# Three routed MLPs of an audio tower: tiles in twos on TensorE, with products ordered by row height

## The reference, cut to what matters

```
l1f, l3f:  Y = (silu(X W_gate) * (X W_up)) W_down          192 -> 2 x 512 -> 192
l3a:       Y = gelu(X W1 + b1) W2 + b2                     192 -> 768 -> 192
```

## Time and profile before

| | |
|---|---|
| device time, median of 3 runs | 2312.69 us (2310.74 to 2312.94) |
| the profiled execution, first to last instruction | 2358.7 us |
| TensorE busy in it | 1698.8 us (72%) |
| VectorE, ScalarE, GpSimd busy | 1290.5 (55%), 1022.7 (43%), 343.4 (15%) |
| mean granted TensorE clock, share of full speed | 0.840 |

### The profile page before, as it was taken

The page is one execution under the profiler, slowest core; times in us unless marked ns, Lnnn a source line. Parts: engine busy times, 40 slices in busy tenths (PEclk is TensorE's granted clock), DMA queues, the critical chain, the costliest instruction groups (busy, mean ns, idle before and its releaser), DMA issues. The chain is left out here.

```text
span 2358.7 us, 35978 instructions
## 1 busy us (share of the span) xinstructions
PE 1698.8 (72%) x12150; PEld 1375.5 (58%) x12166; DVE 1290.5 (55%) x2688; ACT 1022.7 (43%) x2115; POOL 343.4 (15%) x415
## 2 busy tenths in 40 slices
PE   3588879856760489966499686664893698469995
PEld 2265657745650355545489563443683598369995
DVE  6588963361137879968622468997316211642223
ACT  4466753312234568865112147873322254312221
POOL 0000000006640000001143100000000342034431
PEclk9799979977885589986699797775996699689998
DMA  3200000214450000000466300000004453446775
GB/s 85 71 18 19 21 23 9 49 50 128 136 164 16 2 7 7 5 1 12 140 214 212 108 4 8 7 4 1 13 1 127 135 179 118 130 139 223 223 218 191
DMA packets 137245, 189.82 MB, mean 80 GB/s; under 512 B 51661, under 2 KB 111213, under 8 KB 137069
## 3 DMA queue, kind: packets, MB, share of 16 engines
q1 hardware_dynamic: 116289, 146.91, 20.3%
q0 software_dynamic: 15360, 36.72, 5.4%
q10 hardware_dynamic: 5420, 3.91, 0.6%
HBM read 150.21 MB, written 33.68 MB: 78 GB/s over the span
## 5 line engine op out<-in xcount | busy, mean ns | idle before, releaser
L989 DVE TENSOR_TENSOR 36_l3f_mlp_hidden<-36_l3f_mlp_gate,36_l3f_mlp_first 128x512 f32<-128x512 f32 x51 | 35.1, 688 | 185.0 <-ACT 36_l3f_mlp_gate L967 101.0
L882 PE MATMUL 36_l3f_mlp_first<-36_l3f_mlp_xT,36_l3f_mlp_w 128*128 128x128 f32 x816 | 101.5, 278 | 1.8 <-issue 1.8
L1245 PE MATMUL 2_performer_p_u<-perf_proj,2_performer_yT 128*87 128x512 f32 (+1 forms) x204 | 94.1, 605 | 10.6 <-DVE 2_performer_arg L1406 9.5
L882 PEld LDWEIGHTS 36_l3f_mlp_first<-36_l3f_mlp_xT,36_l3f_mlp_w 128*128 128x128 f32 x816 | 96.9, 195 | 2.1 <-issue 2.1
L1005 DVE TENSOR_SCALAR 9_l0f_mlp_y<-9_l0f_mlp_second,l0f_routing_weight 128x192 f32<-128x192 f32 x51 | 20.4, 416 | 142.0 <-PE 9_l0f_mlp_second L896 64.4
L967 ACT ACTIVATE 36_l3f_mlp_gate<-36_l3f_mlp_first 128x512 f32<-128x512 f32 x51 | 30.5, 597 | 136.4 <-PE 36_l3f_mlp_first L887 127.4
L1003 DVE TENSOR_TENSOR 32_l3a_mlp_y<-32_l3a_mlp_second,l3a_experts_b_rows 128x192 f32<-128x192 f32 x29 | 10.4, 358 | 136.7 <-issue 106.3
L896 PE MATMUL 36_l3f_mlp_second<-l3f_experts_w,36_l3f_mlp_hidden 128*128 x408 | 81.0, 342 | 0.0
L989 DVE TENSOR_TENSOR 22_l1f_mlp_hidden<-22_l1f_mlp_gate,22_l1f_mlp_first 128x512 f32<-128x512 f32 x29 | 19.9, 687 | 105.8 <-ACT 22_l1f_mlp_gate L967 78.2
L963 ACT ACTIVATE 32_l3a_mlp_hidden<-32_l3a_mlp_first,l3a_experts_b_cols 128x128 f32<-128x128 f32 x174 | 48.1, 377 | 65.5 <-PE 32_l3a_mlp_first L887 47.6
L2618 ACT ACTIVATE l1a_p<-14_pla_f,l1a_recip 128x87 int16<-128x87 f32 x272 | 71.7, 354 | 9.2 <-DVE l1a_recip L2693 9.2
(11 more groups left out here) (914 smaller groups left out, 4964.0 us busy)
## 6 DMA issues: line engine op xcount, KB each, us to landing
36_l3f_mlp_w<-in_L_ffn_w_dram SPq DMA_DIRECT2D x51, 768.0 KB
22_l1f_mlp_w<-in_L_ffn_w_dram SPq DMA_DIRECT2D x29, 768.0 KB
32_l3a_mlp_w<-in_L_attn_W_dram SPq DMA_DIRECT2D x29, 576.0 KB
9_l0f_mlp_w<-in_L_ffn_down_w_dram SPq DMA_DIRECT2D x51, 192.0 KB
l3a_experts_w<-in_L_attn_W_dram SPq DMA_DIRECT2D x8, 576.0 KB
l1a_blocks<-l1a_qkb SPq DMA_DIRECT2D x192, 5.4 KB, 1.8
l1f_experts_w<-in_L_ffn_w_dram SPq DMA_DIRECT2D x8, 384.0 KB, 6.1
l2a_blocks<-l2a_qkb SPq DMA_DIRECT2D x192, 5.4 KB, 1.8
```

Of the source, the lines that this page charges most:

```text
L882: nc.tensor.matmul(to(t + a * PAIRS), of[:, t + a * PAIRS, :], at[:, 0, :], start=(t == 0), stop=True, skip_group_check=True)
L989: v.tensor_tensor(hidden[j % 2][:], gate[j % 2][:], first[j % 2][1][:, 0, 0:HT, :], ALU.mult).then_inc(hidden_done, 1)
L1245: ins = t.matmul(p_u[:, k, 0:(EIGHT - h) * M], yT[b % 2][:, k, :], proj[:, h:EIGHT, :].rearrange("p h m -> p (h m)"), start=True, stop=True)
```

## The change

A new function, `paired_mlp_stage`, takes the place of `routed_mlp_stage` in l1f, l3a and l3f. The fourth routed MLP (l0f) stays with the old one. Tiles are taken in twos (j, j + 1); an odd last tile is alone. On TensorE a step is now: read both expert numbers; products over 128 rows of j, then of j + 1; products over 64 rows of j, then of j + 1; turn j + 2 and j + 3; second products of the two tiles of the step before. The first two tiles are turned ahead of the loop, and the second products of the last step come behind it. Within a tile every product, operand and destination is the same. ScalarE's order becomes: activation of j, take out j + 2 and j + 3, activation of j + 1. VectorE's becomes: multiply j and j + 1, then the results of the two tiles of the step before. The weights of the first layer have NW = 6 buffers instead of 3, `xT` and `hidden` KEEP = 4 instead of 2; the PSUM buffers stay two. POOL's queue is as before.

```diff
+def paired_mlp_stage(kit, what, route, ex, func, low=False, g=None, b=None, ahead=None, beside=None):
+    NX, NY, NW, LAG, KEEP = 16, 4, 6, 12, 4
+    steps = [range(j, min(j + 2, T)) for j in range(0, T, 2)]
+    after = [range(min(s.stop, T), min(s.stop + 2, T)) for s in steps]
...
+            def whole_rows(j):
+                pe.wait_ge(xT_ready, j + 1)
+                pe.wait_ge(loaded[j % NW], 16 * LOADS * (j // NW + 1))
+                if j >= 2:
+                    pe.wait_ge(hidden_done, j - 1)
...
+            for s, now in enumerate(steps):
+                for j in now:
+                    expert[j] = pe.value_load(route.expert[0:1, j:j + 1], min_val=0, max_val=E - 1)
+                for j in now:
+                    whole_rows(j)
+                for j in now:
+                    half_rows(j)
+                for j in after[s]:
+                    turn(j)
+                for j in steps[s - 1] if s else ():
+                    project(j, expert[j])
+            for j in steps[-1]:
+                project(j, expert[j])
...
+            for j in steps[0]:
+                take_rows(j)
+            for s, now in enumerate(steps):
+                activate(now[0])
+                for j in after[s]:
+                    take_rows(j)
+                for i in now[1:]:
+                    activate(i)
...
-        routed_mlp_stage(kit, "l1f_mlp", route, ex, ACT.Silu, low=True)
+        paired_mlp_stage(kit, "l1f_mlp", route, ex, ACT.Silu, low=True)
...
-        routed_mlp_stage(kit, "l3a_mlp", route, ex, ACT.Gelu, g=gb3[:, 0, :], b=gb3[:, 1, :],
+        paired_mlp_stage(kit, "l3a_mlp", route, ex, ACT.Gelu, g=gb3[:, 0, :], b=gb3[:, 1, :],
...
-        routed_mlp_stage(kit, "l3f_mlp", route, ex, ACT.Silu,
+        paired_mlp_stage(kit, "l3f_mlp", route, ex, ACT.Silu,
```

166 lines of the change are left out of this document (added).

## The result

The changed kernel takes 2295.77 us (median of 5 runs, 2295.07 to 2306.15) against 2312.94 us before (median of 5, 2310.74 to 2318.09): 17.2 us less. The ratio over all runs is 0.9935 with a 95% interval of 0.9916 to 0.9954; it is not the ratio of the two medians, and by it the saving is 15.0 us (10.6 to 19.4). The kernel is faster by clearly more than 0.2%. The median lies in the range of the prediction (2295 to 2316), but only 0.8 us above its lower end, and the saving is 6.6 us larger than the 10.6 us forecast by the medians, 4.4 us by the ratio.

The account below looks back on a forecast made before the run. TensorE's queue was taken to bound l1f, l3a and l3f; 15.3 us saved in the queue plus 0.7 at the end minus 5.4 at the opening gave 10.6 us less, 2312.7 to 2302.1 us, 80% range 2295 to 2316.

Parts of the forecast that it names:

- What bounds the stages: Inner stretches of l1f, l3a, l3f: TensorE's queue alone sets the pace, busy all 462 us at full clock.
- Seam of the 64-row groups and step down: Between a pair's tiles: 64-row groups share a slot, 0.00 instead of 0.21 us; next L882 follows after 0.112 instead of 0.20.
- the lower bound of 9.5 us: Queue saving over 53 pairs if the second tile's 64-row group needs a slot of its own, 0.11 us.
- The saving in the queue: Fewer passages between 128 and 64 rows on TensorE: 0.29 us a pair, 53 pairs, 15.3 us saved.
- The opening: First steps lack second products to cover ScalarE: waits of 1.0 us in l1f and l3f, 3.4 in l3a, 5.4 us lost.
- The end: Last second products no longer wait for their activation: 0.2 us each in l1f and l3f, 0.34 in l3a; 0.7 us saved.
- Carrying the saving over from a span of 2358.7 us: Span 46.0 us above the median; saving taken over whole, as it lies in TensorE's array, not in what a profile adds.
- A: Rival: six weight loads lengthen the opening burst and TensorE creeps, 21 us lost, 2323 us; chance 0.09.
- B: Rival: deeper buffers or new order free the openings of creeping, at most 4 us a stage, 2290 us; chance 0.06.
- the creeping: Opening of l1f: TensorE creeps for over 2 us before the bulk of L887; l3a and l3f look alike.
- C: Rival: TensorE's reports arrive later in the denser stream, waits a pair cost 11 us, 2313 us; chance 0.10.
- D: Rival: the edge belongs to each new tile or operand, not height; saves 0 to 5 us, 2312 to 2318; chance 0.05.

Follow-up runs that it names:

- the transposes between: Kernel before with the next tile's two transposes moved between the 64-row products and second products in l1f, l3a, l3f; 2311.20 us, ratio 0.9976.
- without the 64-row products: Kernel before with the products over 64 rows left out in l3f alone, its last MLP incomplete; one execution, 2252.09 us, not compared.
- second profile: Kernel before, unchanged, profiled again; span 2315.9 us against 2358.7 us in the first profile.
- changed, again: The changed kernel with nothing altered, run again on one chip with three other kernels; 2298.68 us, ratio 0.9917 to the kernel before.
- the buffers alone: Kernel before with six first-layer weight buffers instead of three in l1f, l3a and l3f, nothing else; 2318.22 us, ratio 1.0008.
- the order undone: Changed kernel with TensorE doing 128 then 64 rows of j, then the same of j+1, all else kept; 2320.18 us, ratio 1.0027.

## Why the prediction came out as it did

**What bounds the stages:** right. TensorE had no idle time in the inner stretches before or after, and undoing the order gave everything back.

**Seam of the 64-row groups and step down:** right, 0.20 and 0.09 us. The shared slot is real; the lower bound of 9.5 us did not occur.

**The saving in the queue, 15.3 us:** too small, and this is the step that failed in size. It counted only the distances between starts at the edges of the groups and took eight second products for 8 x 0.176. They are 0.10 + 8 x 0.163: the first one behind 64 rows lasts 0.10 us longer, and the group's mean had spread that over all eight. Before, it was paid twice a pair; now a transpose pays 0.06 once. (The rows on record hinted at it: the two transposes last 0.44 us behind 64 rows in rows 8 and 0.38 elsewhere in rows 3.) That is 0.15 us a pair, so a pair saves 0.45 in l1f and l3f (39 pairs, 17.6 us) and 0.44 in l3a (14, 6.2 us): 23.8 us instead of 15.3. The experiments with the transposes between and without the 64-row products show the term by itself. The lengths of the eight products one by one show it too; the kernel before, second profile, one group of eight in l3f (durations in ns, shortest, median, longest):

```profile
L896 PE MATMUL 36_l3f_mlp_second<-l3f_experts_w,36_l3f_mlp_hidden x8: 326/327/431, 2154.5 to 2155.8; 128*128 x8
```

One product of the eight lasts 0.43 us and the others 0.33.

**The opening, 5.4 us:** the waits were right in kind, 3.0 us in l3a (3.4 forecast), 0.4 and 0.7 in l1f and l3f (1.0 each), 4.1 in all. Two costs were missing. The read of the expert numbers was costed at nothing because 2.8 us of second products lie ahead of it; in the first step nothing does, and it cost 0.9 us a stage, 2.8 in all. And in two of the stages TensorE lost more at half clock, 1.2 GHz, in which each opening begins; the changed kernel in l1f, columns as in rows 2:

```profile
1150.00:1152.00 2.00, 2.00 (x11) 2.00 (x11) 0.00 (x0) 0.00 (x0) 1.39 (x3) 0.50 1.01 415
```

32 products over 128 rows took 6.21 us in l1f where full clock makes 3.67, against 3.13 for 16 where it makes 1.88, so 2.5 us lost instead of 1.3. In l3f it was 2.8 instead of 1.9, but in l3a 1.9 instead of 2.5: 1.6 us more in the three stages. That term is not a steady one, for in "changed, again" the three stages lost 5.4 us in this way, 0.2 less than before. The sum is 4.1 + 2.8 + 1.6 - 0.7 = 7.8 us given back where the forecast had 5.4 - 0.7 = 4.7; the stages say 23.8 - 15.9 = 7.9. So the two misses were of opposite sign, 8.5 us too little saved and 3.1 too little given back, and the total, 5.4 us off, came out nearer than its main term. That is luck, and it is what kept the forecast near the measured time.

**The end, 0.7 us:** right by the rows: the last 24 second products of l1f take 4.17 us without an idle row. (With 0.163 us a product the waits before come to about 0.3 us in each stage, 0.9 in all, a little more than forecast.)

**Carrying the saving over from a span of 2358.7 us:** it did no harm, but the reason given was wrong. The 46 us were not what a profile adds, since the span of the second profile lies 2.1 us under that execution's own time of 2317.99.

**The rivals.** A fell. In l3f the longer burst is there, and TensorE ran through it, first at half and then at full clock; the changed kernel, columns as in rows 2:

```profile
2047.00:2048.00 1.00, 1.00 (x6) 1.00 (x6) 0.00 (x0) 0.00 (x0) 0.83 (x1) 0.50 1.02 381
2048.00:2049.00 1.00, 1.00 (x10) 0.88 (x10) 0.00 (x0) 0.00 (x0) 0.69 (x2) 0.99 1.04 404
2049.00:2050.00 1.00, 1.00 (x20) 1.00 (x20) 0.00 (x0) 0.00 (x0) 0.37 (x1) 1.00 1.06 374
```

B fell with the buffers alone, and the creeping that it priced is not there in the second profile of before. C did not occur: no wait in the inner stretches. D fell with the order undone, which has the same tiles and operands as the changed kernel and 9.14 us a pair, and with the step sums of the kernel without 64-row products.

## What to carry to other kernels

In a TensorE-bound loop, count the passages between full-height and half-height products and order independent tiles so that they share one; a passage down and up costs 0.39 us here, as much as three and a half instruction slots of 0.112 us, and neither busy time nor the mean length of a group shows it. Where TensorE is not the bound, as in l0f, the same order brings nothing. When a loop is grouped more coarsely, cost its first step by itself: each read and each wait that steady work covers stands bare there.

## What the runs showed of the hardware

A change from products over 128 rows to 64 rows delays the next start by 0.09 us; the change back delays it by 0.20 us and lengthens the product that follows by 0.10 us (a transpose by 0.06), the same in all three stages and in every kernel here that has such a change. Only this pair of heights was measured, and why a passage costs what it does, and costs a transpose less, no run shows. Products on opposite halves of the rows share a slot of 0.112 us across tiles and PSUM buffers as they do within one. The Trainium skill, TensorEngine Tiling (Array Packing), section Key Properties, says that a change of tiling mode drains TensorE, without a figure; these are figures for this kernel's float32 products of 128 columns. Of the 0.20 us, one slot of 0.11 is the last 64-row product's own, in which by rows 4 only one half of the array is at work; what is left, 0.09 us, is as much as on the way down. Reading two numbers into TensorE's registers cost about 0.9 us where nothing queued covered it. And one execution of an unchanged kernel was 43 us longer than another, two thirds of it in a single stage that depends on POOL's indirect transfers; its cause is open.
